# A two-layer attention and expert kernel: eight weight chunks are quantised in an earlier stage, and the gathered results are fetched and added by halves

## The reference

```
x = x + grouped_attention(layernorm(x), ctx, ctx)               # 32 query heads, 8 key heads
h = layernorm(x)                                                # routed experts
probs = softmax(h @ classifier.T)                               # 8 experts and 4 zero experts
idx = top_k(probs + bias, 2); rw = probs[idx] * 1.5
x = x + sum over the 2 picks of rw * (down_e(silu(gate_e h) * up_e h)  or  h for a zero expert)
x = x + latent_attention(layernorm(x), ctx)                     # 16 heads, rotary, softmax over 128 keys
h = layernorm(x)                                                # feed-forward 256 -> 1024 -> 256
g, u = q_act(h) @ q_w(w_gate).T, q_act(h) @ q_w(w_up).T
x = x + q_act(silu(g) * u) @ q_w(w_down).T
```

## Time and profile before

| | |
|---|---|
| Three timed runs | 885.82, 889.00 and 889.97 us, median 889.0 |
| The profiled execution | 886.12 us, of which 884.3 us are the span that the trace shows |
| Granted TensorE clock, mean | 0.919 |
| Busy, share of the span | PE 78%, DVE 74%, POOL 66%, PEld 54%, ACT 47% |
| Tile steps, first transpose to the last result copied out | 204.90 to 309.49 us |
| Latent steps 0 to 8, 8 to 24, 24 to 31 | 129.87, 216.07 and 78.82 us |

### The profile page before, as it was taken

How to read it: one execution, slowest core, us unless ns; L and a number is a source line. 1 busy time by engine, 2 the same in 40 slices (tenths; PEclk the granted TensorE clock), 3 DMA queues, 4 the chain that set the end, 5 groups by cost and what they waited for, 6 DMA issues and landing times. The chain is left out here.

```text
span 884.3 us, 14445 instructions
## 1 busy us (share of the span) xinstructions
PE 693.9 (78%) x4502; PEld 481.6 (54%) x4509; DVE 656.0 (74%) x1155; ACT 413.1 (47%) x1115; POOL 587.6 (66%) x631
## 2 busy tenths in 40 slices
PE   4999999611877708879797888999888999975775
PEld 2555555300766607656575655766556677652554
DVE  5899999491677425676659888999899675839995
ACT  1788887304444402435353335344354445444553
POOL 5676775126588244767677886777776778726886
PEclk9999999755999957989899999999999999989999
DMA  9100001242246314313010000000000000000001
GB/s 269 75 1 0 0 1 43 80 182 71 75 133 131 93 59 155 108 56 101 19 43 25 1 19 1 1 20 1 1 1 1 1 1 1 1 1 7 25 29 38
DMA packets 20129, 41.30 MB, mean 47 GB/s; under 512 B 3343, under 2 KB 14223, under 8 KB 19447
## 3 DMA queue, kind: packets, MB, share of 16 engines
q1 hardware_dynamic: 16058, 30.94, 10.5%
q0 software_dynamic: 3456, 9.44, 4.4%
q10 hardware_dynamic: 549, 0.08, 0.1%
HBM read 30.88 MB, written 9.57 MB: 46 GB/s over the span
## 5 line engine op out<-in xcount | busy, mean ns | idle before, releaser
L1860 POOL TENSOR_TENSOR q<-turned 64x512 f32<-64x512 f32 x128 | 167.3, 1307 | 28.1 <-DVE turned L1781 13.8
L1538 PE MATMUL ps<-l_yt,a 128*128 128x512 f32 x576 | 155.8, 420 | 34.6 <-ACT p L1686 34.6
L1538 PEld LDWEIGHTS ps<-l_yt,a 128*128 128x128 f32 x576 | 108.8, 197 | 64.1 <-ACT p L1686 40.0
L1686 ACT ACTIVATE p<-ps,l_negmax 128x128 f32<-128x128 f32 x256 | 91.2, 383 | 82.2 <-DVE l_negmax L1772 82.2
L1847 POOL TENSOR_TENSOR p<-p,l_inverse 128x512 f32<-128x512 f32 x64 | 67.2, 1055 | 86.1 <-DVE l_inverse L1803 76.7
L1781 DVE TENSOR_TENSOR turned<-ps,rope 128x1024 f32<-128x1024 f32 x64 | 77.9, 1217 | 27.8 <-PE ps L1538 26.0
L487 DVE TENSOR_REDUCE negmax<-ps 128x4 f32<-128x512 f32 x128 | 84.3, 684 | 13.6 <-PE ps L310 13.0
L403 ACT ACTIVATE pt<-ps 128x512 f32<-128x512 f32 x128 | 71.2, 599 | 6.9 <-PE ps L332 4.4
L1793 DVE TENSOR_TENSOR turned<-ps,rope 64x512 f32<-64x512 f32 (+1 forms) x96 | 65.6, 683 | 3.4 <-PE ps L1538 2.1
L1578 PE MATMUL ps<-wc,cs 128*128 128x256 f32 x384 | 62.9, 301 | 1.4 <-DVE cs L1809 1.4
L1703 ACT ACTIVATE qs<-ps 128x512 f32<-128x512 f32 x32 | 19.1, 598 | 91.6 <-PE ps L1554 91.6
(11 more groups left out here) (264 smaller groups left out, 1613.0 us busy)
## 6 DMA issues: line engine op xcount, KB each, us to landing
wide<-in_wide SPq DMA_DIRECT2D x8, 768.0 KB, 4.3
slot_rows<-e_out SPq DMA_DIRECT2D x20, 256.0 KB, 2.2
x<-in_x SPq DMA_DIRECT2D x4, 512.0 KB, 8.6
wraw<-in_gate_up SPq DMA_DIRECT2D x2, 1024.0 KB, 19.3
ctx_t<-in_ctx_t SPq DMA_DIRECT2D x1, 2048.0 KB, 7.7
out<-x SPq DMA_DIRECT2D x16, 128.0 KB, 1.7
mx_raw<-in_mx SPq DMA_DIRECT2D x4, 384.0 KB, 7.1
narrow<-in_narrow SPq DMA_DIRECT2D x8, 192.0 KB, 3.4
```

The lines of the kernel that those rows point to most:

```text
L1538: out = pe.matmul(tile_bank(n, k), a[i][:, pa, kin, k * 128:(k + 1) * 128], yt[j % 2][:, py, kin, :, :].rearrange("p b s -> p (b s)"), sta ...
L1686: t = act.activation(p[:, head, s, :], scores_bank(n, head)[:, s * S:(s + 1) * S], ACT.Exp, bias=negmax[:, head, s:s + 1], accum_out=total ...
L1860: t = pool.tensor_tensor(out[rows[(head + half) % 2], head, :], turned[rows[head], half, :], turned[rows[head], 2 + half, :], ALU.add)
```

## The change

- `MX_EARLY` is gone. All 16 chunks are quantised in the tile steps, one in each of steps 0 to 15: `shift(n)` and then `powers(n + 1)` on DVE, `multiply(n)` and then `divide(n + 1)` on POOL. `scale` and `inverse` are doubled, and powers(c) waits for multiply(c - 2). The latent steps hold no quantiser, and PE's waits for it there are gone.
- ACT scales x one sequence a tile step, behind `keep_out`, instead of all before the steps. A one-column Silu (`warm`) stands ahead of the steps.
- PE reads four column offsets in one load in every second step, instead of two loads of one in each.
- On POOL a step's part of `rotate_context` stands behind the gathers, multiply and divide instead of ahead of them. Group 0 is still rotated before the gathers, the other three in the steps. The loads for it (`ctx_t` of 2 MB and five tables) are issued in `turn_rows`, ahead of the store of its rows, instead of at the start of `routed_experts`.
- `fetch` and `combine` go by halves of a group (two sequences, both picks) instead of by picks. In the latent steps a half is fetched at the head of a step on POOL, waited for behind `normalise`, and combined on DVE in the same step; the next half follows in the next step, the statistics in the third.

```diff
-        powers_in = lambda n: (n - 1) // 2 if n % 2 == 1 and (n - 1) // 2 < MX_EARLY else None
-        shift_in = lambda n: (n - 2) // 2 if n % 2 == 0 and 0 <= (n - 2) // 2 < MX_EARLY else None
-        turn_in = lambda n: (n - 4) // 2 if n % 2 == 0 and 0 <= (n - 4) // 2 < MX_EARLY else None
+        shift_in = lambda n: n if n < MX_CHUNKS else None
+        powers_in = lambda n: shift_in(n + 1)
+        turn_in = lambda n: n - 2 if 0 <= n - 2 < MX_CHUNKS else None
...
-                if inside(i, TILE_STEPS):
-                    for t in range(2):
-                        columns[2 * i + t] = pe.value_load(r.column[0:1, 2 * i + t:2 * i + t + 1], min_val=0,
-                                                           max_val=(EXPERTS - 1) * WIDTH)
+                if inside(i, TILE_STEPS) and i % 2 == 0:
+                    _, columns[2 * i:2 * i + 4] = nc.values_load_multi_w_load_instructions(
+                        r.column[0:1, 2 * i:2 * i + 4], engines=[mybir.EngineType.PE], min_val=0,
+                        max_val=(EXPERTS - 1) * WIDTH)
...
-            act.wait_ge(affine, 4)
+            act.activation(warm[:, :], m.eps[:, :], ACT.Silu)
             act.wait_ge(routed.rows_stored[3], 32)
-            for n in range(B):
-                act.activation(m.x[:, n, :], m.x[:, n, :], ACT.Identity, bias=offset[:, n, :],
-                               scale=factor[:, n, :]).then_inc(x_scaled, 1)
             keep_rows(0)
             for n in STEPS:
                 keep_rows(n + 1)
                 keep_gated(n - 1)
                 gates(n)
                 keep_out(n - 1)
+                scale_x(n - 1)
...
+            mx.powers(dve, 0)
             split_rows(0)
             for n in STEPS:
                 split_rows(n + 1)
                 split_gated(n - 1)
                 product(n)
+                if shift_in(n) is not None:
+                    mx.shift(dve, shift_in(n))
                 if powers_in(n) is not None:
                     mx.powers(dve, powers_in(n))
-                if shift_in(n) is not None:
-                    mx.shift(dve, shift_in(n))
...
             for tile in range(GATHERS):
+                if tile == GATHERS // 2:
+                    mx.divide(pool, 0)
                 gather(tile)
...
             for n in STEPS:
-                rotate(ROTARY_STEPS + n)
                 for t in range(2):
                     gather(GATHERS + 2 * n + t)
+                if shift_in(n) is not None:
+                    mx.multiply(pool, shift_in(n))
                 if powers_in(n) is not None:
                     mx.divide(pool, powers_in(n))
-                if shift_in(n) is not None:
-                    mx.multiply(pool, shift_in(n))
+                rotate(ROTATED * ROTARY_STEPS + n)
...
-        wait(dve, self.made, c)
+        wait(dve, self.made, c - 1)
...
-                if group_in(n, 2) is not None:
-                    routed.combine(dve, m, group_in(n, 2), rows_in_slots)
+                for half in range(2):
+                    if group_in(n, half) is not None:
+                        routed.combine(dve, m, group_in(n, half), half, rows_in_slots)
+                if group_in(n, 2) is not None:
                     routed.statistics(dve, m, group_in(n, 2))
-                if chunk_in(n, 0) is not None:
-                    mx.powers(dve, chunk_in(n, 0))
-                if chunk_in(n, 1) is not None:
-                    mx.shift(dve, chunk_in(n, 1))
...
             for n in RUN:
+                for half in range(2):
+                    if group_in(n, half) is not None:
+                        routed.fetch(pool, group_in(n, half), half, rows_in_slots)
                 normalise(n - 2, 0)
                 normalise(n - 2, 1)
+                for half in range(2):
+                    if group_in(n, half) is not None:
+                        routed.wait_fetched(pool, group_in(n, half), half)
                 add(n)
                 if group_in(n, 3) is not None:
                     deviations(group_in(n, 3))
-                for k in range(TOP_K):
-                    if group_in(n, k) is not None:
-                        routed.fetch(pool, group_in(n, k), k, rows_in_slots)
-                        routed.wait_fetched(pool, group_in(n, k), k)
-                if chunk_in(n, 0) is not None:
-                    mx.divide(pool, chunk_in(n, 0))
-                if chunk_in(n, 1) is not None:
-                    mx.multiply(pool, chunk_in(n, 1))
```

More of the change, by code:

```diff
@@ L46 @@
 ROTARY_STEPS = 5
-MX_CHUNKS, MX_EARLY = 16, 8
+MX_CHUNKS = 16
 SLOT_TILES = 40
@@ L697, in turn_rows @@
         PAIRS, FIRST = 2, 2 * GROUPS - 2
-        y = [sb(f"y_rows{i}", [S, 2, E]) for i in range(PAIRS)]
+        y = [scope.enter_context(nc.sbuf_tensor(f"y_rows{i}", [S, 2, E], F32, side="right")) for i in range(PAIRS)]
         y_ps = [m.ps[:, 2 + i, :].rearrange("p (k b s) -> p k b s", k=HALVES, b=2) for i in range(PAIRS)]
@@ L1079, in keep_out, with scale_x @@
                     act.activation(out[i % STORES], out_ps[i % 2], ACT.Copy).then_inc(out_kept, 1)
+            def scale_x(n):
+                if inside(n, B):
+                    if n == 0:
+                        act.wait_ge(affine, 4)
+                    act.activation(m.x[:, n, :], m.x[:, n, :], ACT.Identity, bias=offset[:, n, :],
+                                   scale=factor[:, n, :]).then_inc(x_scaled, 1)
             act.wait_ge(routed.table_loaded, 16)
@@ L1221, in _ @@
                              table(TABLE_S + 1, 1).to_broadcast([S, ZERO * B])).then_inc(slots_filled, 1)
-            for k in range(ROTARY_STEPS):
+            for k in range(ROTATED * ROTARY_STEPS):
                 rotate(k)
@@ L1248, in _ @@
             pool.wait_ge(slot_made, 1)
-            for k in range(TOP_K):
-                routed.fetch(pool, 0, k, rows_in_slots)
-            for k in range(TOP_K):
-                routed.wait_fetched(pool, 0, k)
+            for half in range(2):
+                routed.fetch(pool, 0, half, rows_in_slots)
+            for half in range(2):
+                routed.wait_fetched(pool, 0, half)
             pool.wait_ge(routed.stats_made, 4)
@@ L1666, in spare @@
                     f.keep(act, fj, rows_ps)
-                if chunk_in(n, 4) is not None and place == 3:
-                    mx.keep(act, m, chunk_in(n, 4), mx_ps)
             def normalise(j):
```

96 lines of the change are left out of this document (41 added, 55 removed).

## The result

The changed kernel takes 841.33 us (median of four runs, 840.28 to 842.47), the kernel before 888.47 us in the same session: a ratio of 0.9473, with a 95% interval of 0.9446 to 0.95. The forecast was 856, with a range of 842 to 876. The profiled execution took 841.84 us with a span of 839.9, so against the profiled execution of before (886.12, on which the sum was built) 44 us are gone where 31 were forecast.

The account below looks back on a forecast made before the run. The latent stage was taken as bound by PE, or by DVE where the quantiser rides along. 886.1 + 15 - 32 - 14 = 855.1 us, put at 856 for a median, with a range of 842 to 876.

Parts of the forecast that it names:

- Term 1: Tile steps: they get longer with all chunks in them, the last copy ending at 324.4 us, 15 us later.
- P: Tile steps: the length of one step holding a chunk, taken as 6.1 us, with bounds of 5.5 and 7.2.
- Term 2: Latent steps 8 to 24: eight quantiser chunks leave, a gain of 32 us, at most 36.
- a plain step: Latent steps: one without the quantiser, PE full; 11.26 us each over steps 24 to 31, 10.88 in the timeline.
- term 3: Latent steps 0 to 8: split multiply-adds and no waits for landed fetches give 116 us, a gain of 14.
- the 19.2 us lost: Latent steps 0 to 8: the part of 129.87 us in which PE is not busy (busy for 110.70).
- Tight and dear tile steps: Two rivals on tile steps: P near 5.5, 846 us, chance 0.15; P near 7.2, 871 us, chance 0.19.
- The slower one: Rival, tile steps: gathers stand still while DVE holds the ports, P = 9.0, 898 us; chance 0.05.
- the latent steps don't speed up: Rival, latent steps: a chain between engines bounds them, the quantiser only fills it, 887 us; chance 0.04.
- the dear rival: Tile steps: P near 7.2 from a further lock wait or PE's clock, 871 us; chance 0.19.

Follow-up runs that it names:

- rotate_between: The changed kernel with POOL's rotation part between multiply and divide in the tile steps: 839.47 us, 0.947 of the kernel before.
- spread_only: The kernel before with only x scaled by ACT one sequence a tile step: 876.41 us, 0.9879 of the kernel before.
- late_chunks: The changed kernel with the quantiser of chunks 8 to 15 put back in the latent steps: 858.05 us, 0.9654 of the kernel before.
- pad_dve: The changed kernel with a shift's five DVE operations added, on unread memory, to every second latent step of 8 to 23: 869.73 us, 0.9807.
- rotated3_fill: The changed kernel with three groups rotated before the gathers, plus eight unread PE transposes in each of steps 2 to 17: 843.18 us, 0.9481.
- picks_back: The changed kernel with fetch and combine by picks again: 858.83 us, 0.9662 of the kernel before.
- halves_only: The kernel before with only fetch and combine changed, to halves: 865.71 us, 0.9764 of the kernel before.
- rotated3_late: The changed kernel with three groups rotated before the gathers and DVE's product moved behind the shift: 833.36 us, 0.9397 of the kernel before.
- one_offset: The changed kernel with the column offsets loaded one by one again: 838.76 us, 0.9473 of the kernel before.
- rotated3: The changed kernel with three context groups rotated before the gathers: 841.03 us, 0.949 of the kernel before.
- early_powers: The changed kernel with three groups rotated before the gathers, the next chunk's powers ahead of the shift, and the product last: 837.78 us, 0.9439.

## Why the forecast was off, point by point

The account is against the profiled executions: 31 us forecast (886.1 to 855.1), 44.3 measured.

- **Term 1, forecast 15 us later, measured 14.5** (324.0 against 309.49). shift(0) ended 2.2 us sooner than the 216.4 forecast, 15 steps took 92.7 us where 15 P were 91.5, and the tail 17.1 instead of 16.5. P = 6.1 was right, its reasons only half, so part of the hit was luck. I put the wait for the ports at the head of the shift, as in the earlier trace rows; there it is 0.51 us now, and the long one is at the powers, 1.37 us. rotate_between shows that it hardly matters which of POOL's operations it meets. And the term hides two of opposite sign: 27.7 us for eight chunks and 13.3 back, nearly all from x being scaled in the steps.
- **Term 2, forecast 32, measured 39.2, and 2.6 more in steps 24 to 31.** This is the step that failed, in its words: "It can't be more than 216.07 - 180.2 = 36". The mechanism was right and the term too small, for two reasons. The measure of a plain step, 11.26 us, was a mean over steps 24 to 31, whose first two (12.0 and 11.4 us, against 9.8 and 11.2 in the changed kernel) still carried work left over from the steps before: PE has 556 matmuls in this window, against 533 in the changed kernel, at the same idle time of 1.4 us and the same clock of 1.00. With the 10.88 of the earlier trace rows the ceiling would have been 42. This is 6.1 of the 7.2 us missed. And the transpositions and the clip, for which I added 2 us each, are partly hidden: 16 steps of 10.88 are 174.1, the measured stretch has 2.7 more, not 4. The 2.6 us of steps 24 to 31, a stage for which the forecast had no term, are where the edge of the window falls: spread_only has the quantiser in steps 8 to 24 and still takes 76.1 us for steps 24 to 31 and 295.3 for 8 to 31 (294.9 before). late_chunks shows that the quantiser is the whole cause.

A second thing the forecast never says: PE's busy time itself falls, here from 191.1 us in these 16 steps to 176.8, at 1250 and 1244 matmuls. Term 2 held this without naming it, since a plain step is one at the upper clock; term 3 left it out. The groups of PE's instructions in steps 8 to 24 show where, first of the kernel before, then of the changed one (columns: count, then busy us and mean ns, then idle time just before them):

```profile
L1538 PE MATMUL ps<-l_yt,a 128*128 128x512 f32 x286 | 78.8, 424 | 25.0 <-ACT p L1686 25.0
L1578 PE MATMUL ps<-wc,cs 128*128 128x256 f32 x192 | 30.7, 295 | 0.0
L1552 PE MATMUL ps<-q,b 128*64 128x512 f32 x64 | 22.9, 802 | 0.0
L1554 PE MATMUL ps<-q,b 128*128 128x512 f32 x32 | 19.4, 689 | 0.0
...
L1318 PE MATMUL ps<-ident,wide 128*128 128x128 bf16 x18 | 2.0, 222 | 0.0
```

```profile
L1529 PE MATMUL ps<-l_yt,a 128*128 128x512 f32 x292 | 72.5, 400 | 0.0
L1569 PE MATMUL ps<-wc,cs 128*128 128x256 f32 x192 | 30.7, 295 | 0.0
...
L1545 PE MATMUL ps<-q,b 128*128 128x512 f32 x32 | 18.0, 645 | 0.0
...
L1543 PE MATMUL ps<-q,b 128*64 128x512 f32 x64 | 17.3, 618 | 0.0
```

All of PE's idle time stands ahead of L1538, and only that group and the two right behind it were slow (424, 802 and 689 ns against 400, 618 and 645), 13 us together; those further on cost the same to the nanosecond. Another 2.0 us are the quantiser's own transposes (L1318). So a stall of PE was paid for twice, as idle time and as matmuls at the lower clock behind it. pad_dve shows it with no quantiser at all: 20.0 us idle and 7.1 more busy. The Trainium skill, page "TensorE: Matmul & The Clock Gate", section "Part 1: The HAM clock gate (the "warmup" mystery)", says that the clock is set by how busy the array has been of late. The trace of pad_dve agrees, with 0.66 behind the stall of 3.77 us; rotated3_fill, where more work left the clock at 0.79, does not bear it out. The numbers were in the earlier trace rows: 191 us busy at a clock of 0.94 are 180 at full clock, and 110.7 at 0.92 are 102; 176.8 and 105.0 were measured.

- **Term 3, forecast 14, measured 18.4.** POOL's waits for a landed fetch went from six, 11.0 us together, to one of 2.8 us. PE's idle time fell by 12.6 us (19.2 to 6.6), near the 14. The rest, 5.7 us, is busy time (110.70 to 104.97), which the forecast took as fixed when it counted only "the 19.2 us lost". picks_back and halves_only show that the part stands alone.
- **Rows not in the forecast:** from the last result to latent step 0 as before (38.65 against 38.76), and latent step 31 to the end 1.4 us longer (112.69 against 111.29), which is within what that unchanged stage varies.
- **The account:** 14.5 - 0.1 - 18.4 - 39.2 - 2.6 + 1.4 = -44.4 us of span. Of the 13 us missed, 7.2 are in term 2, 4.4 in term 3, 2.6 in steps 24 to 31, 0.5 in term 1, and -1.4 at the end.
- **The rivals.** Tight and dear tile steps: P was neither. The slower one falls: the gather with the shift beside it lasts 1.12 to 1.23 us in rotated3_late, 0.95 alone. The rule of the Trainium skill on it (page "SBUF — State Buffer", section "SBUF: two separate sides") is borne out here by 0.3 us at most. That the latent steps don't speed up falls with PE's 176.84 of 176.84 us. The clock, which I named for the dear rival and argued away from the feed-forward's share, did fall to 0.82; it cost nothing at P = 6.1 (in one_offset it was 0.87 in the same window, and the multiplies stood 6.11 us apart), and was the bound in every second step of rotated3, where the others took 5.2 us.
- **Smaller points.** DVE's busy time is 33 us lower (656.0 to 623.4), as forecast. The four offsets a load, credited with "something", are worth nothing measurable.

What stays open: why the clock did not rise with the filler (PE busy for 52.8 of 66 us), while in late_chunks, with PE busy for 47.3 of 65.0 us, and in rotated3_late, with 30.6 of 45.0 us from 255 us on, it was 1.00. No run here tells that apart.

## What to carry to other kernels

When a change takes away stalls of TensorE, its busy time isn't a floor: multiply it by the granted clock of the stretch, and take as the gain the idle time and this difference (an estimate that came within 3% here, twice). Take the measure of an undisturbed step from the shortest ones well away from the disturbed stretch, not from a mean that begins at its edge. A stage in which three engines hand work round in a ring is shortened by taking a link off the ring (the product behind the shift, 8 us between rotated3 and rotated3_late), not by filling a wait that the profile shows on one of them (0 us in rotate_between, and early_powers was no faster).

## What the runs showed of the hardware that was not expected

- A stall of PE of 1.91 us left the ten matmuls behind it at 2.74 us; behind one of 2.57 they took 4.28, and behind one of 3.77, 4.31.
- Eight more transposes a step on PE (busy 52.8 us instead of 49.7 in 66) left the granted clock at 0.79; it had been 0.78.
- Sixteen POOL products of 0.85 us in a stage where DVE was busy for 126 of 177 us and PE for all of them cost nothing (176.59 against 176.84).
- Added to DVE alone in the same stage, five operations a chunk lasted 711, 1321, 1509, 1526 and 1096 ns beside POOL's additions, where in the tile steps the same operations take 352 to 557 at their shortest.
- The stage behind latent step 31 is the same in the changed kernel and its variants, and its length varied from 108.7 to 112.7 us between their profiled executions. A difference of 2 to 3 us in the total of one execution says little; the windows by stage say more.
